# Attention of an adaLN block: from bf16 pieces on the whole array to 32-row groups of two fp32r pieces

## What is computed

```python
q = (x @ wq).reshape(B, T, H, D)
lat = x @ w_down
k = (lat @ wk_up).reshape(B, T, H, D)
v = (lat @ wv_up).reshape(B, T, H, D)
q, k = _apply_rope(q, cos, sin), _apply_rope(k, cos, sin)
scores = jnp.einsum('bqhd,bkhd->bhqk', q, k) * scale
pages = jnp.arange(T) // PAGE_SIZE                 # pages of 32
allowed = pages[None, :] <= pages[:, None]
scores = jnp.where(allowed[None, None], scores, jnp.finfo(scores.dtype).min)
attn = jax.nn.softmax(scores, axis=-1)
out = jnp.einsum('bhqk,bkhd->bqhd', attn, v).reshape(B, T, E) @ wo
```

## Time and profile before

| | |
|---|---|
| median of 3 runs | 770.15 us |
| the profiled execution's own time | 771.94 us |
| its span | 770.1 us, 12222 instructions |
| TensorE matmul (PE) | 681.2 us busy, 88% |
| VectorE (DVE) | 588.5 us, 76% |
| ScalarE (ACT) | 520.4 us, 68% |
| GpSimd (POOL) | 183.8 us, 24% |
| chain that ended last | PE 33%, DVE 12%, issue 5% of the span |

### The profile page before, as it was taken

How to read it: one execution, slowest core, us unless ns; L and a number is a source line. 1 busy time by engine, 2 the same in 40 slices (tenths; PEclk the granted TensorE clock), 3 DMA queues, 4 the chain that set the end, 5 groups by cost and what they waited for, 6 DMA issues and landing times.

```text
span 770.1 us, 12222 instructions
## 1 busy us (share of the span) xinstructions
PE 681.2 (88%) x3976; PEld 427.2 (55%) x4000; DVE 588.5 (76%) x1133; ACT 520.4 (68%) x905; POOL 183.8 (24%) x144
## 2 busy tenths in 40 slices
PE   3920988999699999987599999999999999999996
PEld 2410222333233333345478777787777877778885
DVE  5670987888588888229678898888988889888775
ACT  2530035677476777973488888888888888888984
POOL 0451016000000000000223343333433344322322
PEclk9965579999899999998799999999999999999998
DMA  9541041100101000000111110011100111101200
GB/s 237 150 139 65 0 117 40 43 21 25 46 2 44 24 20 4 3 1 1 66 45 55 56 56 28 29 56 56 55 34 24 54 56 57 54 2 55 69 15 28
DMA packets 17413, 37.20 MB, mean 48 GB/s; under 512 B 3305, under 2 KB 11241, under 8 KB 14533
## 3 DMA queue, kind: packets, MB, share of 16 engines
q1 hardware_dynamic: 16037, 34.65, 13.9%
q10 hardware_dynamic: 1312, 1.74, 0.9%
HBM read 31.86 MB, written 4.33 MB: 47 GB/s over the span
## 4 chain that ended last, share of the span: by engine, by line
PE 33%; DVE 12%; issue 5%; ACT 1%; POOL 0%; POOLq 0%; DVEq 0%
DVE gel_lo L1049 6%; PE y L952 6%; PE y L954 5%; PE y L953 5%; PE hid L943 5%; PE hid L942 5%; PE hid L941 5%; PE plog L963 2%; DVE part L1105 1%; ACT gel_hi L1017 1%; DVE at_least L1077 1%; PE pcw L972 1%; DVE cw L1096 0%; DVE cw L1094 0%; DVE dl L1084 0%
## 5 line engine op out<-in xcount | busy, mean ns | idle before, releaser
L1049 DVE TENSOR_TENSOR gel_lo<-gel,gel_hi 128x512 fp32r<-128x512 f32 x256 | 248.3, 1010 | 6.7 <-ACT gel_hi L1017 5.7
L588 DVE TENSOR_REDUCE mcol<-mx 128x1 f32<-128x512 f32 (+2 forms) x320 | 193.1, 635 | 61.7 <-PE mx L704 58.8
L562 ACT ACTIVATE probs<-st 128x512 f32<-128x512 f32 x288 | 155.7, 596 | 99.3 <-PE st L660 57.1
L1016 ACT ACTIVATE gel<-hid,b_sb 128x512 f32<-128x512 f32 x256 | 176.1, 688 | 38.5 <-PE hid L943 16.2
L1017 ACT ACTIVATE gel_hi<-hid,b_sb 128x512 fp32r<-128x512 f32 x256 | 174.7, 682 | 0.0
L1157 POOL TENSOR_TENSOR cur<-cur,part 128x512 f32<-128x512 f32 x64 | 106.4, 1663 | 250.8 <-DVE part L1105 250.8
L704 PE MATMUL mx<-ks,qs 125*128 125x512 bf16 (+3 forms) x384 | 120.8, 364 | 38.3 <-PEq L208 32.0
L952 PE MATMUL y<-gel_hi,w_hi 128*128 128x512 f32 x256 | 104.4, 408 | 0.4 <-DVE gel_lo L1049 0.2
L941 PE MATMUL hid<-cur_hi,w_hi 128*128 128x512 f32 x256 | 102.2, 399 | 0.4 <-DVE cur_lo L1123 0.4
L943 PE MATMUL hid<-cur_hi,w_lo 128*128 128x512 f32 x256 | 102.2, 399 | 0.0
L942 PE MATMUL hid<-cur_lo,w_hi 128*128 128x512 f32 x256 | 102.1, 399 | 0.0
(11 more groups left out here) (147 smaller groups left out, 521.9 us busy)
## 6 DMA issues: line engine op xcount, KB each, us to landing
cwb<-gate_rows SPq DMA_DIRECT2D x16, 1024.0 KB, 4.7
ks<-in_k_rows SPq DMA_DIRECT2D x3, 640.0 KB
qs<-in_q_rows SPq DMA_DIRECT2D x3, 616.0 KB
q_pieces<-pieces_q SPq DMA_DIRECT2D x4, 384.0 KB, 4.8
k_pieces<-pieces_k SPq DMA_DIRECT2D x4, 384.0 KB, 6.0
ks<-k_pieces SPq DMA_DIRECT2D x8, 192.0 KB
qs<-q_pieces SPq DMA_DIRECT2D x8, 192.0 KB
x_sb<-in_x SPq DMA_DIRECT2D x4, 256.0 KB, 5.2
```

The costliest lines, as they stand in the source:

```text
L562: nc.scalar.activation(probs[u % SLOTS][:, h, :], st[:, (HG * u + h) % ST_RING, :], ACT.Exp, scale=SCALE).then_inc(exp_done, 1)
L588: nc.vector.tensor_reduce(mcol[a % SLOTS][:, h, slot:slot + step * (len(blocks) - 1) + 1:step], mx[:, at % MX_RING, 0:len(blocks) * keys]. ...
L1016: nc.scalar.activation(gel[n % RING][:, :], hid[n % RING][:, :], ACT.Gelu_apprx_tanh, bias=bias)
L1049: nc.vector.tensor_tensor(gel_lo[n % RING][:, :], gel[n % RING][:, :], gel_hi[n % RING][:, :], ALU.subtract).then_inc(lo_ok, 1)
```

## The change

The attention is written anew for two fp32r pieces (`hi` + `lo`) in place of three bf16 ones.

- q and k need 24 rows per head (three products of pieces), then 2 rows of the maximum and 4 rows that mask the pages of the own block of 128 keys: at most 30 rows. The 4 heads of a group lie in the four groups of 32 partitions of one tile of 128 x 1024, so a matmul uses 24 to 30 rows of the array. Where a block of 128 is the own one, it is a matmul of its own with 30 rows (`cut`). That makes 18 matmuls per head and group for the scores and 18 for the bins, where there were 12 and 12. The columns are the same, 4608 per head for each.
- `quad` issues, piece by piece in turn, the scores of heads 0 and 1 and a bin of heads 2 and 3, then the other way round. A bin now holds two heads, and VectorE reads 1024 columns at once: 20 reads per group. There are 2 such double banks.
- There are 10 units per group (two of them 256 wide) in place of 9. `weigh` is issued once per unit, not in halves, one unit behind the scores. The sum has one bank in place of two.
- GpSimd cuts the maxima in two (`take_apart`, 2 steps); they go into `qs` by four DMAs in place of one.
- The loop is gone; all 80 units are written out.
- In `prep` each piece is stored once for each product (24 stores of 256 KB in place of 8 of 384 KB), GpSimd makes one subtraction per side in place of two, ScalarE's second copy is gone, the constant rows are sent once into device memory, and a group is loaded by 2 DMAs of 512 KB in place of 6. `prep` no longer waits for the stores of batch 1; the wait stands in `attention` ahead of the first maxima rows. Group 2 is loaded behind the feed-forward weights.

The diff, cut to its core:

```diff
...
-Q_PIECE = [0, 0, 0, 1, 1, 2]
-K_PIECE = [0, 1, 2, 0, 1, 0]
+Q_PIECE = [0, 0, 1]
+K_PIECE = [0, 1, 0]
...
-ROW_MAX = P - 3
+HROWS = 32
+ROW_MAX = TERMS * D
+ROW_PAGE = ROW_MAX + 2
+ROW_END = ROW_PAGE + 4
...
-    [(0, 0, 0, 0, 512)],
-    [(1, 0, 0, 0, 512)],
-    [(0, 2, 0, 256, 256), (1, 6, 256, 256, 256)],
...
+    (0, [(0, 0, 0, 512)]),
+    (0, [(1, 0, 128, 384), (3, 384, 384, 128)]),
+    (0, [(2, 0, 256, 256)]),
+    (1, [(0, 0, 0, 512)]),
+    (1, [(1, 0, 0, 512)]),
+    (1, [(2, 0, 0, 512)]),
+    (1, [(3, 0, 0, 512)]),
+    (1, [(4, 0, 0, 512)]),
+    (1, [(5, 0, 128, 384), (7, 384, 384, 128)]),
+    (1, [(6, 0, 256, 256)]),
 ]
 NU = len(UNITS)
...
+def cut(rows, own_rows, blocks):
+    pieces = []
+    for at, off, first, width, own, own_first in blocks:
+        for r, x, w in ((own_rows, 0 if own_first else width - own, own), (rows, own if own_first else 0, width - own)):
+            if w:
+                pieces.append((r, at, off + x, first + x, w))
+    return pieces
+SCORE_PIECES = [cut(ROW_PAGE, ROW_END, [(j, off, q0, nq, P if j // TPC == c else 0, True) for j, off, q0, nq in blocks])
+                for c, blocks in UNITS]
+BIN_PIECES = [cut(ROW_MAX, ROW_END, [(t, x * keys, k0, keys, P if k0 + keys == (t + 1) * P else 0, False)
+                                     for x, (t, k0) in enumerate(blocks)])
+              for blocks, keys, _, _ in BINS]
+MOST_PIECES = max(len(p) for p in SCORE_PIECES + BIN_PIECES)
...
-            m.qs = [ma.sb(f"qs{s}", [P, HG, T], BF16) for s in range(SLOTS)]
+            m.ks = [ma.sb(f"ks{s}", [P, T], F32R) for s in range(SLOTS)]
+            m.qs = [ma.sb(f"qs{s}", [P, T], F32R) for s in range(SLOTS)]
             m.qk_in = [ma.sem(f"qk_in{s}") for s in range(SLOTS)]
...
 def load_group(sp, m, g, s):
-    for first, n in LOADS:
-        rows = slice(first * D, (first + n) * D)
-        sp.dma_start(m.ks[s][rows, :, :],
-                     m.kp[0:n, g].rearrange("c (d h) t -> c d (h t)", d=D)).then_inc(m.qk_in[s], 16)
-        one = m.qp[Q_PIECE[first]:Q_PIECE[first] + 1, g].rearrange("c (d h) t -> c d (h t)", d=D)
-        sp.dma_start(m.qs[s][rows, :, :], one.broadcast_to([n, D, HG * T])).then_inc(m.qk_in[s], 16)
+    for dst, src in ((m.ks[s], m.kp), (m.qs[s], m.qp)):
+        sp.dma_start(dst[:, :].bitcast(F32), src[g].rearrange("h r t -> (h r) t")).then_inc(m.qk_in[s], 16)
...
                     n = 2 * c + side + 1
+                    rows = dst[b * NG:(b + 1) * NG].rearrange("g h r t -> (g h) r t")
                     sp.wait_ge(piece0, n)
                     sp.wait_ge(piece1, n)
-                    sp.wait_ge(piece2, n)
-                    sp.dma_start(dst.rearrange("c g r t -> (g r) c t")[b * P:(b + 1) * P, :, at],
-                                 pieces[side][:, c, :, :]).then_inc(pieces_out, 16)
+                    for term, x in enumerate(which):
+                        sp.dma_start(rows[:, D * term:D * (term + 1), at],
+                                     pieces[side][:, c, x, :].bitcast(F32)).then_inc(pieces_out, 16)
                 if c == 1:
-                    sp.wait_ge(pieces_out, 16 * 4)
+                    sp.wait_ge(in_rows, 32)
+                    sp.wait_ge(pieces_out, 16 * 4 * TERMS)
                     load_group(sp, m, 0, 0)
                     load_group(sp, m, 1, 1)
-            sp.wait_ge(in_rows, 16 * SLOTS * 2)
-            sp.wait_ge(pieces_out, 16 * NCH * 2)
...
-                    pool.wait_ge(rest, n + 1)
-                    nc.gpsimd.tensor_tensor(pieces[side][:, c, 2, :], rr[side][:, :], pieces[side][:, c, 1, :],
-                                            ALU.subtract).then_inc(piece2, 1)
+                    pool.wait_ge(piece0, 2 * c + side + 1)
+                    nc.gpsimd.tensor_tensor(pieces[side][:, c, 1, :], ro[side][:, c % 2, :], pieces[side][:, c, 0, :],
+                                            ALU.subtract).then_inc(piece1, 1)
...
-    ST_RING, MX_RING = 3, 3
...
+            def max_rows(g):
+                s = g % SLOTS
+                sp.wait_ge(bin_read, turn_at(g) + 1)
+                for h in range(HG):
+                    n = 2 * JB
+                    sp.dma_start(m.qs[s][HROWS * h + ROW_MAX:HROWS * h + ROW_MAX + 2, :].bitcast(F32),
+                                 mrow[n * h:n * (h + 1), :]).then_inc(mrow_in[s], 16)
...
+            load_group(sp, m, 2, 2)
+            sp.wait_ge(m.pieces_out, 16 * NCH * 2 * TERMS)
+            for g in range(GROUPS):
+                max_rows(g)
+                if g >= 1 and g + 2 < GROUPS:
+                    sp.wait_ge(st_done, HG * NU * g)
+                    load_group(sp, m, g + 2, (g + 2) % SLOTS)
...
+            def take_apart(g):
+                mc = mcol[g % 2]
+                nm = mc[:, :, 0:JB]
+                hi, lo = mpc[:, :, 0, :], mpc[:, :, 1, :]
+                pool.wait_ge(mchain, CHAIN * g + 1)
+                if g >= 1:
+                    pool.wait_ge(bin_full, turn_at(g - 1) + 1)
+                nc.gpsimd.tensor_copy(hi.bitcast(F32R), nm).then_inc(mchain, 1)
...
+            def exps(k, h):
+                u = k % NU
+                n = sum(b[3] for b in UNITS[u][1])
+                act.wait_ge(st_done, HG * k + h + 1)
+                if h == 0 and k >= PROBS:
+                    act.wait_ge(pv_done, k + 1 - PROBS)
+                nc.scalar.activation(probs[k % PROBS][:, h, 0:n], st[:, (HG * k + h) % ST_RING, 0:n], ACT.Exp,
+                                     scale=SCALE).then_inc(exp_done, 1)
...
+            def merge(g):
+                mc = mcol[g % 2]
+                v.wait_ge(bin_read, bin_at(g, NBINS - 1) + 1)
+                nc.vector.tensor_tensor(mc[:, :, 4:8], mc[:, :, 4:8], mc[:, :, 8:12], ALU.min).then_inc(mchain, 1)
+            for g in range(GROUPS):
+                for n in range(NBINS):
+                    if n == 1 and g >= 1:
+                        merge(g - 1)
+                    if n == TURN_AFTER and g >= 1:
+                        keep_rows(g - 1)
+                    read_bin(g, n)
...
+            def score_room(k, h):
+                g, u = divmod(k, NU)
+                n = HG * k + h
+                if u == 0:
...
+                if n >= ST_RING:
+                    pe.wait_ge(exp_done, n + 1 - ST_RING)
+            def score(k, h, x):
+                g, u = divmod(k, NU)
+                s, n, r0, c = g % SLOTS, HG * k + h, HROWS * h, UNITS[u][0]
+                rows, j, off, q, w = SCORE_PIECES[u][x]
+                mm = nc.tensor.matmul(st[:, n % ST_RING, off:off + w], m.ks[s][r0:r0 + rows, j * P:(j + 1) * P],
+                                      m.qs[s][r0:r0 + rows, c * CH + q:c * CH + q + w], start=True, stop=True)
+                if x == len(SCORE_PIECES[u]) - 1:
+                    mm.then_inc(st_done, 1)
+            def bin_room(g, n):
+                at = bin_at(g, n)
+                if n == 0:
+                    pe.wait_ge(m.qk_in[g % SLOTS], 32 * uses(g))
+                if at >= MX_RING:
+                    pe.wait_ge(bin_read, at + 1 - MX_RING)
+            def bin_piece(g, n, x):
+                s, at = g % SLOTS, bin_at(g, n)
+                b, pair = divmod(n, PAIRS)
+                rows, t, off, k0, w = BIN_PIECES[b][x]
+                for i in range(2):
+                    r0 = HROWS * (PAIR_HEADS[pair] + i)
+                    mm = nc.tensor.matmul(mx[:, at % MX_RING, i, off:off + w], m.qs[s][r0:r0 + rows, t * P:(t + 1) * P],
+                                          m.ks[s][r0:r0 + rows, k0:k0 + w], start=True, stop=True)
+                if x == len(BIN_PIECES[b]) - 1:
+                    mm.then_inc(bin_full, 1)
+            def fill_bin(g, n):
+                bin_room(g, n)
+                for x in range(len(BIN_PIECES[n // PAIRS])):
+                    bin_piece(g, n, x)
+            def quad(k, pair):
+                g, u = divmod(k + NU + LEAD, NU)
+                n = PAIRS * u + pair
+                score_room(k, 2 * pair + 1)
+                if g < GROUPS:
+                    bin_room(g, n)
+                for x in range(MOST_PIECES):
+                    for h in (2 * pair, 2 * pair + 1):
+                        if x < len(SCORE_PIECES[k % NU]):
+                            score(k, h, x)
+                    if g < GROUPS and x < len(BIN_PIECES[n // PAIRS]):
+                        bin_piece(g, n, x)
...
+                pe.wait_ge(exp_done, HG * (k + 1))
...
                     for h in range(HG):
-                        mm = nc.tensor.matmul(ov[32 * h:32 * h + 32, c, q0 + lo - off:q0 + hi - off],
-                                              vs[s][:, j, h, :], probs[u % SLOTS][:, h, lo:hi],
...
+            def turn_maxima(g):
+                at = turn_at(g)
+                pe.wait_ge(mchain, CHAIN * (g + 1))
+                pe.wait_ge(bin_read, at + 1 - MX_RING)
+                nc.tensor.transpose(mx[0:HG * 2 * JB, at % MX_RING, 0, 0:P],
```

(63 more changed lines are left out.)

343 lines of the change are left out of this document (87 added, 256 removed).

## The result

The changed kernel takes **840.49 us** (median of 4 runs, 839.68 to 841.74) against 770.26 us for the kernel before beside it (769.77 to 772.15): a ratio of 1.0908, 95% interval 1.0884 to 1.0932. The prediction was 720.6, with 702 to 760 as its range. It is wrong, on the wrong side of no change.

The account below looks back on a forecast made before the run. TensorE was taken to bound the scores, VectorE the maxima ahead of them. From 770.1 us, 21.2 (start), 1.7 (maxima) and 26.6 (scores) were subtracted to give 720.6 us; the range was 702 to 760.

Parts of the forecast that it names:

- Preparation: Stage before attention: uniform loads and quicker store issues let attention start at 54.2 us, 21.2 us earlier.
- SyncE's queue drains first: Rival in the preparation: stores issue only as the queue drains, attention starts at 61, total 727 us; chance 0.09.
- Maxima: Stage of maxima ahead of the scores, bound by VectorE: 30.0 us for 31.7, 1.7 us gained.
- Row groups overlap: Scores: matmuls of four heads in four row groups run side by side, 0.24 us per step of a quad.
- Weights go in one by one: Rival in the scores: weight loads run serially, a group takes 29.5 us, total 750 us; chance 0.15, in part or whole.
- row groups don't overlap: Rival in the scores: a quad takes 0.96 us, a group 33, total 779; chance 0.08 shared with clock low for most.
- The price of a quad: Scores: one step 0.24 us, or 0.1 if 128 wide, 0.30 for a mean quad.
- The way to ScalarE: Scores: fill of 0.45 us from a quad's start to the first exponential.
- The clock drops: Rival in the scores: 1.2 GHz, 37.5 us per group, 814 us if it stays; chance 0.12 for a part.

Follow-up runs that it names:

- e5b_row_burst: The changed kernel with 20 steps of four side-by-side 26-row matmuls right ahead of the first unit of scores; 847.8 us.
- e12_tail_three: e9_no_burst without the one whole-array matmul ahead of the first quad in the last 14 units, three left ahead of the second; 742.64 us, ratio 0.9649.
- e9_no_burst: e10_tail without the burst of 20 matmuls ahead of the loop, its whole-array matmuls between the quads kept; 747.12 us.
- e2_fill: e1_burst with one extra whole-array matmul of 512 columns ahead of the quads (156 of the 160); 804.12 us.
- e1_burst: The changed kernel with 20 whole-array matmuls of 512 columns, results overwritten, right ahead of the first unit of scores; 844.39 us.
- e11_one_fill: e10_tail with one whole-array matmul instead of two ahead of the second quad in the 66 units before the last 14; 858.55 us.
- e10_tail: e7b_fill_hidden with one whole-array matmul ahead of the first and three ahead of the second quad in the last 14 units; 750.43 us, ratio 0.9734.
- e7b_fill_hidden: e2_fill with the same 156 extra matmuls, but two ahead of each unit's second quad and none ahead of the first; 756.61 us, ratio 0.980.

## Why the prediction was wrong

**Preparation: right**, 54.65 for 54.2, but in part by another way. SyncE was to be free at 49 and VectorE last at 53.1; in fact twelve issues took 10.3 us, not 4.4, and ended at 53.96, while VectorE was done at 49.8. Two errors cancelled, so the time was hit by luck. The rival *SyncE's queue drains first* had the mechanism half right and the size wrong.

**Maxima: right**, 31.0 for 30.0; first score at 85.68 for 84. But VectorE's readings were put at 20.5 us per group and took 177.3/8 = 22.2 (L567): reading 1024 columns at once saved nothing over two readings at 0.60, it takes 1.23.

**Row groups overlap: right.** All four start within 0.01 us (217.92), and their weights with them. *Weights go in one by one* and *row groups don't overlap* fall, the second with 0.23 us for a step of four in e5b_row_burst.

**The price of a quad: too low.** A step was set at 0.24 from the chained matmuls of the net, a mean `quad` at 0.30. In a chain that is right. But a `quad` stands between matmuls of other tilings, and its first weights lie open: at full clock 0.43 for one step and 0.49 with two pieces. The way to ScalarE was set at 0.45 and is 0.53 to 0.58. One plain unit of e12_tail_three, from `quad` to `quad`:

```profile
212.81 0.50 PE L612 MATMUL st<-qs,ks 26*128 26x512 f32 x2
...
214.00 0.49 PE L612 MATMUL st<-qs,ks 26*128 26x512 f32 x2
...
214.49 1.06 PE L680 MATMUL ov<-probs,vs 128*32 128x512 f32 x8
215.48 0.50 PE L612 MATMUL st<-qs,ks 26*128 26x512 f32 x2
```

That is 1.19 + 0.49 + 0.99 = 2.67, where the sum in the prediction gave 2.49 and 2.55 was put down.

**The clock: the step that failed.** The sum of the scores was made at 2.4 GHz throughout. *The clock drops* was a rival, priced at 37.5 us per group for 40.2 measured, and its full form, 814 us, had with "no overlap" a chance of 0.08. Two reasons were given against it. The first, that 1.0 was held over 17 us of the projection, is from a stretch with TensorE busy 15.68 of 17 us in a dense chain of whole-array matmuls, which is another pattern than the one priced; and in the same stage the clock was at 0.5 from 360.0 to 366.8, just behind that window. The second, "`weigh` keeps its four passes", is refuted by the kernel after itself: it keeps them and runs them at 0.50 for 322 us. The row that was like the new stage was the earlier trace rows, 75.4 to 107.1, with TensorE busy 28.9 of 31.7 us on maxima with waits, at 0.50. The change put a pattern like it in place of the dense one; that likeness is an argument, and no run compares the two. The two places in the scores of the kernel before where the clock fell, 127.9 and 203.0, look different: TensorE had had little to do for some microseconds, 0.97 us busy in the four before the first. The windows view of the second:

```profile
200.00:206.40 6.40, 1.12 (x19) 0.58 (x18) 1.52 (x3) 1.38 (x3) 0.40 (x1) 0.73 0.29 72
```

In the kernel after no wait of TensorE in the scores is over 0.9 us by the profile, and the clock is low all the same.

That the clock is the cause is shown by e9_no_burst and e12_tail_three: the loop of the kernel after, with two whole-array matmuls per unit put in, turns in 27.1 us in place of 40.2; and by e2_fill, where one loop ran at both levels. What the same kernel would do at 2.4 GHz without them, no run shows, since none held the clock without them. As an estimate: in a plain unit they cost nothing, 1.19 from `quad` to `quad` with them (above) and 1.20 without (e1_burst, 93.05 to 94.25); where a `quad` has two pieces it is 1.32 with them (e12_tail_three, 199.52 to 200.84). If all ten units gained that 0.12 the group would be 25.9, if none did 27.1, so it lies in between, beside 25.8 predicted. By that the clock costs 13.1 to 14.3 us per group, 105 to 114 of the shortfall of 118.6, and 2.7 behind the scores; the rest is 1.5 in the first two stages and up to 10 in a sum of the scores that was too low, in the `quad`, the way to ScalarE and VectorE's readings. By the same estimate the time at full clock would have been above 720.6, but inside the range.

**Why two fills per unit raise it and one does not** stays open. Gapless work on row groups raised it, TensorE busy all the time with one fill did not, and with two the rise came 7 to 65 us after the fall or the start, differently with the same number of fills. Work that kept a high clock in one run (e9_no_burst) did not raise a low one for 55 us in another (e11_one_fill). Useless matmuls on row groups in the same wait were not run. Which of columns, rows or gaps it goes by was not separated.

## What to carry to other kernels

A stage that takes work off TensorE for the same answer may halve its clock too: price every such change at both clocks, give the low one a chance according to the stretch of the trace that looks most like the new pattern, and take the granted clock, not the busy share, as the evidence. Where TensorE waits in a fixed place of a loop, useless whole-array matmuls put into that wait, and only there, can pay for themselves many times: here 98 us. Count each change between tilings as one weight load that nothing hides, here 0.2 us at full clock.

## What was not expected of the hardware

- TensorE busy 39.95 of 40 us at a granted 0.50, for 317 us on end (e11_one_fill), and, with one more matmul of some 0.4 us per unit, 1.00 after 24 us (e10_tail).
- The clock rose 3.2 us into a burst of whole-array matmuls and 6.8 us into one on row groups; it was gone 6.8 and 3.4 us after the rise.
- Equal fills, unequal delays: the clock came back after 6.8 us in e7b_fill_hidden and after 23.9 us in e10_tail, which are the same up to the end of the stage. The six executions of e10_tail spread from 748.17 to 758.04 us, those of the kernel after from 839.68 to 841.74. Their mean granted clocks fit a rise that comes late by chance: 0.939 in the two of 757.57 (the profiled one) and 758.04 us, 0.950 in the four of 748.17 to 751.11.
- A weight load of 128 fp32 columns is 0.18 to 0.19 us at 2.4 GHz and 0.28 to 0.33 at 1.2 GHz, side by side in four row groups.
